# Two sets of edits together in a fused wavelet-attention and mixture-of-experts kernel: front stages and search rounds; tables, gathers and scatters

## The reference, cut to what matters

```
x = x + attn_block(layernorm(x));  x = x + moe(layernorm(x))        # both in f32
attn_block: two levels of depthwise 4-tap convolutions with stride 2 (low band by h_filter, high band by
  g_filter); linear attention with 16 heads of 8 channels on the lowest band (q = k = elu + 1); two levels
  of synthesis (repeat by 2, then depthwise 4-tap convolutions, low + high); layer norm of (x + low)
moe: h = 2048 x 128; scores = sigmoid(h @ gate_w.T)                 # 16 experts
  each expert takes the 256 tokens with its highest scores (top_k over the tokens, ids kept)
  xin = h[topk_ids]; eo = (silu(xin @ gw.T + gb) * (xin @ up_w.T + up_b)) @ down_w.T + down_b
  out = zeros.at[topk_ids].add(eo * topk_score) + shared           # 512 hidden columns per expert
  shared = (silu(h @ sh_gate.T) * (h @ sh_up.T)) @ sh_down.T        # 256 hidden columns, all tokens
```

## Time and profile before

| | us |
|---|---|
| median of 3 runs (242.78 to 243.35) | 243.33 |
| the profiled execution's own time | 241.03 |
| its span, first to last instruction | 239.3 |
| PE busy | 190.8 (80%) |
| DVE busy | 126.6 (53%) |
| POOL busy | 124.1 (52%) |
| ACT busy | 93.6 (39%) |
| POOL scatters L430, 32 of them | 50.9 |
| POOL gathers L418, 32 of them | 31.6 |

### The profile page before, as it was taken

How to read it: one execution, slowest core, us unless ns; L and a number is a source line. 1 busy time by engine, 2 the same in 40 slices (tenths; PEclk the granted TensorE clock), 3 DMA queues, 4 the chain that set the end, 5 groups by cost and what they waited for, 6 DMA issues and landing times.

```text
span 239.3 us, 3513 instructions
## 1 busy us (share of the span) xinstructions
PE 190.8 (80%) x1166; PEld 159.2 (67%) x1166; DVE 126.6 (53%) x450; ACT 93.6 (39%) x226; POOL 124.1 (52%) x155
## 2 busy tenths in 40 slices
PE   7369899999975886839578999999998888999100
PEld 7354787999862354527366899999988778889100
DVE  3679546489664788877833444444443433444000
ACT  1375301041979646611203444444444344344100
POOL 7310000035310434370987887787778877665660
PEclk9979999999996799976999999999999999999755
DMA  6999992000008300101022332333223333322331
GB/s 212 407 418 417 416 416 98 3 1 3 0 8 212 153 3 1 45 0 44 3 69 59 83 49 38 45 51 48 40 42 49 47 47 34 37 22 22 26 29 11
DMA packets 11584, 22.18 MB, mean 93 GB/s; under 512 B 1456, under 2 KB 8752, under 8 KB 11440
## 3 DMA queue, kind: packets, MB, share of 16 engines
q1 hardware_dynamic: 5936, 17.52, 19.2%
q0 software_dynamic: 5632, 4.46, 14.4%
HBM read 17.65 MB, written 4.33 MB: 92 GB/s over the span
## 4 chain that ended last, share of the span: by engine, by line
PE 39%; DMA 16%; DVE 13%; POOL 13%; issue 8%; ACT 7%; POOLq 1%; SPq 0%; DVEq 0%
DMA out_dram<-area,rows 12%; POOL out_dram L430 8%; PE bank L966 7%; PE bank L1215 5%; PE bank L1104 4%; PE bank L1216 4%; DVE junk L786 4%; PE bank L1198 4%; DMA x_tok<-in_x_dram 3%; PE bank L946 3%; POOL hT L418 2%; ACT hrow L463 2%; POOL sh_hid L404 2%; PE bank L1012 2%; DVE search L804 1%
## 5 line engine op out<-in xcount | busy, mean ns | idle before, releaser
L430 POOL DMA_INDIRECT out_dram<-area,rows x32 | 50.9, 1589 | 18.4 <-DMA out_dram<-area,rows 10.2
L912 DVE SCALAR_TENSOR_TENSOR area<-bank,consts,sgate 128x256 f32<-128x256 f32 x64 | 30.8, 481 | 34.9 <-ACT sgate L596 34.9
L596 ACT ACTIVATE sgate<-bank,consts 128x256 f32<-128x256 f32 x64 | 30.0, 468 | 45.9 <-PE bank L1216 45.9
L1215 PE MATMUL bank<-area,wT 128*128 128x256 f32 x128 | 39.4, 390 | 4.9 <-issue 4.0
L1198 PEld LDWEIGHTS bank<-wT,area 128*128 128x128 f32 x256 | 38.3, 191 | 3.2
L384 POOL TENSOR_TENSOR rstd<-var_eps,half_pow 128x4 f32<-128x4 f32 (+1 forms) x10 | 12.5, 1249 | 50.4 <-DVE var_eps L622 50.4
L1198 PE MATMUL bank<-wT,area 128*128 128x128 f32 x256 | 38.6, 275 | 0.0
L1216 PE MATMUL bank<-area,wT 128*128 128x256 f32 x128 | 38.1, 379 | 0.0
L418 POOL DMA_INDIRECT hT<-h_rows,rows x32 | 31.6, 986 | 9.5 <-issue 9.2
L404 POOL TENSOR_TENSOR sh_hid<-sh_up,sgate 128x128 f32<-128x128 f32 x32 | 16.9, 559 | 30.1 <-ACT sh_up L564 19.1
L1216 PEld LDWEIGHTS bank<-area,wT 128*128 128x128 f32 x128 | 24.4, 190 | 3.3
(11 more groups left out here) (181 smaller groups left out, 263.3 us busy)
## 6 DMA issues: line engine op xcount, KB each, us to landing
wT<-in_weights_dram SPq DMA_DIRECT2D x16, 768.0 KB, 18.1
h_rows<-hrow SPq DMA_DIRECT2D x2, 576.0 KB, 3.5
x_tok<-in_x_dram SPq DMA_DIRECT2D x2, 512.0 KB, 5.2
x_tok<-in_down_b_dram SPq DMA_DIRECT2D x1, 1024.0 KB, 6.7
out_dram<-x SPq DMA_DIRECT2D x4, 256.0 KB, 2.2
hT<-h_rows,rows POOLq DMA_INDIRECT x32, 2.6
out_dram<-area,rows POOLq DMA_INDIRECT x32, 3.4
sh_wT<-in_shared_dram SPq DMA_DIRECT2D x1, 384.0 KB, 7.4
```

The costliest lines, as they stand in the source:

```text
L430: pool.indirect_dma_start(out=out_rows, in_=eo[:, e % 2, c, :], in_offset=None, out_offset=bass.IndirectOffsetOnAxis(ap=rows[:, g, c, k:k ...
L596: act.activation(sgate_e[:, q % SGB, :], up_bank(q)[:, CAP:2 * CAP], ACT.Silu, bias=biasT[:, 1, j, e:e + 1]).then_inc(s_sil, 1)
L912: dve.scalar_tensor_tensor(hidden[:, e % 2, j, :], up_bank(q)[:, 0:CAP], biasT[:, 0, j, e:e + 1], sgate_e[:, q % SGB, :], ALU.add, ALU.mul ...
L1215: pe.matmul(up_bank(q)[:, 0:CAP], wT[:, e, 0, j, :], xselT[:, e % 2, :], start=True, stop=True)
```

## The change: what it does, and the diff

**Loads.** SP waits for the second half of x before it issues the shared weights and all that follows.

**Front.** The high band of level one is computed by PE for sequence 0 alone; DVE computes it for sequence 1 (`high1`, four operations, of the forms of L663 and L665). DVE finishes `h2p` before it waits for `kv`. PE's order changes: `add_xn` moves ahead, level one of the synthesis is done by sequence (`synth1_even(b)` in banks 4 and 7), and groups 0 and 1 of level two come before sequence 1's odd part. `turn_x1(0)` moves in between groups 2 and 3. The warm-up matmuls are (0, 8, 8, 0) in place of (8, 8, 2, 4). ACT makes `features` for group 0 alone.

**Search rounds.** The other 12 tiles of `hrow` are made by DVE, one in each of rounds 0 to 11 (`norm_tiles([4 + r], ...)`). `features_T` of groups 1 to 3 runs in rounds 3, 7 and 11, `keep_hT` in rounds 4, 8 and 12. SP stores each half of `hrow` when its tiles are there.

**Tables.** The slots are written in f16 and transposed with an f16 identity. `shared_down(2)` moves ahead of that transpose. POOL no longer multiplies or adds group 3 of the shared part: DVE multiplies it (`s_lasthid`, between `slot_rows(0)` and `own_expert(1)`) and adds it to x1 ahead of `keep_x(0)` (`s_lastbase`).

**Gathers and scatters.** POOL issues 10 chunks, then for each expert `scatter(e)` and behind it as many single chunks as `BETWEEN[e]` says.

```diff
+    AHEAD = 5
+    BETWEEN = (2, 2, 1, 2, 2, 1, 2, 2, 1, 2, 2, 1, 2, 0, 0, 0)
...
             load_x(1)
+            sp.wait_ge(s_x[1], 16)
             sp.dma_start(sh_wT[:, :, :], shared).then_inc(s_shw, 16)
...
             for b in range(NB):
-                sp.wait_ge(s_hna, 2 * (b + 1))
+                sp.wait_ge(s_hna, 1)
+                sp.wait_ge(s_hnv, 1 + 2 * b)
...
-            for n in range(LAST + 1):
+            for n in range(LAST):
                 for t in range(SHT):
...
+            shared_add(LAST - 1)
...
-            for e in range(GBUF - 1):
-                gather(e)
-                if e == 3:
-                    shared_add(LAST)
+            for e in range(AHEAD):
+                for c in range(CH):
+                    gather(e, c)
+            chunk = AHEAD * CH
             for e in range(E):
-                if e + GBUF - 1 < E:
-                    gather(e + GBUF - 1)
                 scatter(e)
+                for _ in range(BETWEEN[e]):
+                    gather(*divmod(chunk, CH))
+                    chunk += 1
...
             normalise_sum(2)
+            keep_x1T(1)
             features(0)
-            keep_x1T(1)
             normalise_sum(3)
-            features(1)
...
-            features(2)
             keep_hT(0)
-            features(3)
...
-                if r in (0, PERIOD, 2 * PERIOD):
-                    keep_hT(1 + r // PERIOD)
+                if r in (4, 8, 12):
+                    keep_hT(r // 4)
             keep_part(len(ROUNDS) - 1)
-            for part in range(4):
+            keep_down(LAST - 1)
+            for part in (0, 2):
                 keep_shared(LAST, part)
-            keep_down(LAST - 1)
-            keep_down(LAST)
...
+            def high1(k):
+                r, o = PHASE[k]
+                dst, src = h1p[:, 1, 1:N1 + 1], xp[:, r, 1, o:o + N1]
+                if k == 0:
+                    return dve.tensor_scalar(dst, src, taps[:, 4:5], None, ALU.mult)
+                return dve.scalar_tensor_tensor(dst, src, taps[:, 4 + k:5 + k], dst, ALU.mult, ALU.add)
...
                     dve.wait_ge(s_dve, step[0])
+                    if r < NT - 4:
+                        last = norm_tiles([4 + r], lambda i: hrow[:, i, 0:C], x1_t)
+                        if r % 4 == 3:
+                            last.then_inc(s_hnv, 1)
                     link(dve.scalar_tensor_tensor(base, ktab, ...))
...
-            slot_gt = score2[:, :]
+            slot_gt, slot_eq = slot_f[:, 0, :], slot_f[:, 1, :]
...
             slot_rows(0)
+            for t in range(SHT):
+                dve.wait_ge(s_shsil, SHT * LAST + t + 1)
+                dve.wait_ge(s_shu, SHT * LAST + t + 1)
+                dve.tensor_tensor(sh_hid[:, LAST % 2, t, :], bank[2 + t][:, :], sgate[:, t, :], ALU.mult).then_inc(s_lasthid, 1)
             own_expert(1)
...
+            dve.wait_ge(s_shout, LAST + 1)
+            last_x1 = x1[:, group(LAST), :].rearrange("p i c -> p (i c)")
+            dve.wait_ge(s_base, LAST)
+            dve.tensor_tensor(last_x1, bank[4][:, :], last_x1, ALU.add).then_inc(s_lastbase, 1)
             dve.wait_ge(s_db_in, 16)
             keep_x(0)
...
+            add_xn(0)
+            add_xn(1)
             pe.wait_ge(s_l2, 1)
...
+            pe.wait_ge(s_apa, 1)
+            synth1_even(1)
+            synth2_low(0)
+            synth2_high(1)
+            synth2_low(1)
             synth1_odd(1, h2p, 9)
-            pe.wait_ge(s_apa, 1)
             synth1_odd(1, ap_, 4).then_inc(s_up2, 1)
-            synth2_high(1)
-            synth2_low(0)
-            synth2_low(1)
-            for n in (2, 3):
-                synth2_high(n)
-                synth2_low(n)
...
+            synth2_high(2)
+            synth2_low(2)
+            turn_x1(0)
+            synth2_high(3)
+            synth2_low(3)
...
+            for t in range(4):
+                shared_down(LAST - 1, t)
             pe.wait_ge(s_pos, 1)
             for r in range(2):
-                pe.matmul(bank[5][:, r * P:(r + 1) * P], score2[:, r:256:2], ident[:, :], start=True, stop=False)
-                last = pe.matmul(bank[5][:, r * P:(r + 1) * P], sel[:, 4, r:256:2], ident[:, :], start=False, stop=True)
+                for k in range(2):
+                    last = pe.matmul(bank[5][:, r * P:(r + 1) * P], slot_f[:, k, r:256:2], ident_h[:, :], start=(k == 0),
+                                     stop=(k == 1))
             last.then_inc(s_posT, 1)
             for t in range(4):
-                shared_down(LAST - 1, t)
                 shared_up(LAST, t // 2, t % 2)
```

More of the change, by code:

```diff
@@ L408, in _, with gather @@
                     shared_add(n - 1)
-            def gather(e):
+            shared_add(LAST - 1)
+            def gather(e, c):
                 g, k = divmod(e, 8)
-                if e % 8 == 0:
+                if e % 8 == 0 and c == 0:
                     pool.wait_ge(s_rows, g + 1)
-                if e >= GBUF:
+                if e >= GBUF and c == 0:
                     pool.wait_ge(s_eo, CH * (e - GBUF + 1))
[L417 to L420, removed]
+                pool.indirect_dma_start(out=gath[:, e % GBUF, c, :], out_offset=None, in_=h_rows[:, :],
+                                        in_offset=bass.IndirectOffsetOnAxis(ap=rows[:, g, c, k:k + 1], axis=0),
+                                        ).then_inc(s_gath[e % GBUF], 16)
             def scatter(e):
@@ L942, in _ @@
             pe.wait_ge(s_diag, 1)
-            for b in range(NB):
-                pe.wait_ge(s_xp, 2 * b + 2)
-                for k, (r, o) in enumerate(PHASE):
-                    last = pe.matmul(bank[4 + b][:, :], diag[:, k, :], xp[:, r, b, o:o + N1], start=(k == 0), stop=(k == 3))
-                last.then_inc(s_h1, 1)
+            pe.wait_ge(s_xp, 2)
+            for k, (r, o) in enumerate(PHASE):
+                last = pe.matmul(bank[4][:, :], diag[:, k, :], xp[:, r, 0, o:o + N1], start=(k == 0), stop=(k == 3))
+            last.then_inc(s_h1, 1)
             def place(n, t):
@@ L979, in synth2_low, with synth1_even, synth1_odd @@
                 synth(n, range(4), r1p, 4).then_inc(s_up1, 1)
+            def synth1_even(b):
+                for k, o in TAPS[0]:
+                    last = pe.matmul(EVEN_BANK[b][:, 0:N2], diag[:, 9 + k, :], h2p[:, b, o:o + N2], start=(k == 0),
+                                     stop=(o == 2))
+                last.then_inc(s_up2h, 1)
+            def synth1_odd(b, band, d0):
+                for k, o in TAPS[1]:
+                    last = pe.matmul(bank[5 + b][:, 0:N2], diag[:, d0 + k, :], band[:, b, o:o + N2],
+                                     start=(d0 == 9 and k == 3), stop=(d0 == 4 and o == 2), skip_group_check=True)
+                return last
+            add_xn(0)
+            add_xn(1)
             pe.wait_ge(s_l2, 1)
@@ L1006, in _ @@
             last.then_inc(s_nd, 1)
-            add_xn(3)
-            synth2_high(0)
-            def synth1_odd(b, band, d0):
-                for k, o in TAPS[1]:
-                    last = pe.matmul(bank[5 + b][:, 0:N2], diag[:, d0 + k, :], band[:, b, o:o + N2],
-                                     start=(d0 == 9 and k == 3), stop=(d0 == 4 and o == 2), skip_group_check=True)
-                return last
+            synth2_high(0, range(2, 4))
             pe.wait_ge(s_h2, 1)
-            pe.wait_ge(s_h1a, 2)
-            for k, o in TAPS[0]:
-                last = pe.matmul(bank[4][:, :], diag[:, 9 + k, :], h2p[:, :, o:o + N2], start=(k == 0), stop=(o == 2))
-            last.then_inc(s_up2h, 1)
+            pe.wait_ge(s_h1a, 1)
+            synth1_even(0)
             synth1_odd(0, h2p, 9)
@@ L1072, in _ @@
             pe.wait_ge(s_gc, 1)
-            for g in range(LAST + 1):
+            for g in range(1, LAST + 1):
+                turn_x1(g)
+                router(g - 1)
                 stay_warm(WARM_T[g], bank[5])
-                turn_x1(g)
-                if g:
-                    router(g - 1)
             last = router(LAST)
```

99 lines of the change are left out of this document (60 added, 39 removed).

## The result

| | before | after |
|---|---|---|
| median, us | 243.34 (4 runs, 242.78 to 243.95) | 251.53 (4 runs, 248.71 to 256.22) |
| the profiled execution's own time | 241.03 | 251.9 |
| its span | 239.3 | 250.1 |

The ratio is 1.0297, with an interval of 1.0207 to 1.0388: slower, as forecast, and by more than forecast (forecast +4.0; measured +8.2 in the medians, +7.2 by the ratio). The two traces stand 10.8 apart, more than the medians, since the execution profiled before was shorter than each of the four runs in the table and the one after is the longest of the three that the ratio uses. What follows explains the traces.

A forecast was written before the change was run, and what follows sets the result against it. It took POOL's full queue of scatters and gathers to bound the longest stretch. Scatter 0 at -13.2, chain +12.0 and PE's clock +5.2 summed to +4.0, a median of 247.3 us, range 240.5 to 252.

The forecast's parts named there:

- Loads, front, scores: Start to ACT's first count: loads -1.7, synthesis -2.3, behind its end -2.6, together -6.6; features leaving ACT after the scores -2.85.
- Rounds: Search rounds: DVE tiles 1.0, copies 0.4 and edges 0.3 against a clock gain of 0.75; sum +1.0, bounds -1 and +4.5.
- a gain of 0.75: First three search rounds: PE sits idle less before them, so its granted clock is less low, -0.75.
- Tables: Last search round to PE's first expert matmul: f16 transposes, earlier rows and POOL's earlier first gather, -2.95.
- the bounds: Tables: -0.5, where PE's clock falls before shared_down(2), and -4.
- Scatter 0: Start of the first scatter: PE's first expert matmul at 115.75 plus 9.85 gives 125.6, 13.2 earlier.
- The chain: Scatter 0 onward: late gathers close a loop behind scatter 9; 103.5 against 91.5, +12.0, plus 5.2 for PE's clock.
- The clock term: Late expert steps: PE's clock halves in idle gaps, doubling its 1.75 in three of four steps; +5.2, bounds 0 and +7.
- together 9.1: Closed loop behind scatter 9: two scatters 3.82, landing 2.55, turn_x to bias 1.84, bias 0.42, ACT 0.4 and signals, 9.1.
- No starvation: Rival for the expert chain: late gathers land before PE asks; chain 90.5, 229 us in all; chance 0.10.
- Its clock stays up: Rival for the expert stretch: gathers starve PE but its clock holds; 242.1 us; chance 0.20.
- the third: Rival: front's gain mostly missing; tiles lengthen rounds by 0.3 each, shared_down(2) meets low clock; 252 us; chance 0.12.

The follow-up runs named there:

- experiment 6: SP's wait for the second half of x, alone in the kernel before: 241.67 us, ratio 0.9951; taken out of experiment 8's kernel: 230.78 us, ratio 0.9543.
- experiment 8: Experiment 1's kernel with nine warm-up matmuls on PE ahead of the first table, run twice: 228.07 us (ratio 0.947) and 229.61 us (0.9498).
- experiment 7: Experiment 1's kernel with features of groups 1 to 3 back on ACT and no DVE tiles in the rounds: 232.03 us, ratio 0.9596.
- experiment 2: The changed kernel with POOL's old order, 12 chunks ahead, then a scatter and two gathers per expert: 231.27 us, ratio 0.9544.
- experiment 5: The changed kernel, POOL's order untouched, with turn_x(e+1) issued one q later, behind the down ending expert e-1: 236.02 us, ratio 0.9801.
- experiment 1: The changed kernel with 12 chunks gathered ahead of scatter 0 in place of 10: 230.98 us, ratio 0.9484.
- experiment 3: The kernel before with only the new order of gathers and scatters (10 ahead, new BETWEEN): 259.92 us, ratio 1.0783.
- experiment 4: The changed kernel with 14 warm-up matmuls on PE ahead of its gather waits for experts 12 to 15: 246.11 us, ratio 1.0184.
- experiment 9: Experiment 8's kernel with a one-column POOL memset taking the waits ahead of scatter 0: 228.81 us, ratio 0.9485.

## Why the prediction was right in its mechanism and low in its sum

**Loads, front, scores: right, one size low.** Forecast: ACT's first count 6.6 + 2.85 = 9.45 earlier. It came at 63.41 in place of 74.08, 10.67 earlier, and the first compare 10.03 earlier:

```profile
62.11 0.40 ACT L553 ACTIVATE area<-bank 128x256 f32<-128x256 f32 x1 [1.03 <-PE bank L1129]
...
63.41 0.52 ACT L568 ACTIVATE below<-area,search 128x256 bf16<-128x256 uint16 x1
```

The scores started at 69.68 before, so 7.57 of it is the front's, against 6.6. DVE's second half of x came 1.80 earlier (forecast 1.7), the exponential 3.54 (21.30 in place of 24.84; forecast 1.7 + 0.95 = 2.65), and that is where most of the surplus lies. My sum treated the terms as independent, which experiment 6 refutes; it held since both edits were in.

**Rounds: forecast +1.0, measured +1.85.** The tiles cost what I took, 0.05 to 0.1 each on the mean: without a second stretch of half clock the rounds take 28.16 with them (experiment 8) and 28.54 - 1.2 without (experiment 7), some 0.8 for 12 tiles. Only the spread was other: 0.5 of it lies in the tenth step, where a tile and the operation behind it met POOL's operations. The rule of "Who interferes with whom" ("SBUF — State Buffer", the Trainium skill), which I had weighed for this term, is what those rows agree with: tiles that meet POOL are 0.58 long, the others 0.34. The remaining 1.1 of the 1.85 is a second stretch of half clock, in the rounds from 74.6 to 79.2 (2.52 and 2.02 where 1.72 and 1.64 are usual). I had booked the clock as a gain of 0.75. It did not come: the first round took 1.73 in place of 1.98, but the granted clock was 0.50 in it and 0.71 in the next, and the first three together took 5.95 against 5.92.

**Tables: forecast -2.95, measured -1.45.** Both parts came: with a warm-up the stage is 21.93, 2.75 below before. What ate 1.3 of it in the kernel after is mostly a late landing, for which my sum had no term. The second gather landed 4.14 behind its issue, against the median of 2.6, and PE, done with the shared part, waited for it:

```profile
112.22 4.14 DMA hT<-h_rows,rows
```

```profile
116.40 0.44 PE L1235 MATMUL bank<-ident,hT 128*128 128x128 f32 x2 [1.17 <-DMA hT<-h_rows,rows]
```

From the first gather to PE's first expert matmul it is 6.82 here and 5.74 in experiment 8's first trace. The half clock that I had put into the bounds was there too, though behind `shared_down(2)` and not ahead of it: PE has nothing from 102.5 to 104.8, and from 105.7 to 110 its granted clock is 0.50. But it was low before the change as well (0.50 from 106 to 110), and experiments 2 and 5, with the same low stretch (0.50 from 108 to 114 and from 105.9 to 111.9) and no late landing, have tables of 22.00 and 22.18. So here it cost 0.2 or so. Why that one landing was late was not tried. POOL's first gather followed its rows, as forecast; but 0.90 behind them, not 0.2 (rows written from 109.51 to 109.80, gather at 110.70).

**Scatter 0: forecast -13.2, measured -10.6.** Rounds 0.85, tables 1.5, less 0.6 from the earlier first compare, make PE's first expert matmul 1.77 later than forecast. The rest, 0.84, is the step from there to the scatter: 10.69 in place of 9.85. The first chunk was ready at 127.34, as long after PE as before; the scatter started at 128.21. Before, POOL was in the middle of its queue then, with 0.30 between two instructions, and I took that for what a waiting POOL would show too.

**The chain: forecast 103.5 + 5.2, measured 112.98.** The mechanism is right at every point: which step is the first long one, which is the longest, what ends PE's wait, and the fall of the clock. Experiments 1, 3, 5 and 4 show its cause (the chunks), its independence of the front, its lock (the place of `turn_x`) and its clock term. The clock term was right in sum, 5.36 against 5.2, by luck and not in its parts: all four steps pay, by 1.03 to 1.49 each, and not three by 1.75. The steps up to scatter 9 took 0.8 more than forecast, of landings that ended late (7.01 in place of 6.42 in one step, behind a scatter that landed after 4.81 where 3.4 is the median), the last two 0.1. What was mis-sized is the fixed part of the loop, "together 9.1": at the full clock it is 9.97 (experiment 4). Of the 0.87, 0.76 is again the start of POOL's indirect DMA, 0.81 behind the first chunk where I had put some 0.05 for signals. Over the four steps the loop without the clock's price took 40.86 where I had 37.7, 3.2 more.

Against the forecast the trace's span is 6.8 longer (250.1 against 243.3): 2.6 up to scatter 0 and 4.3 in the chain. Of this 3.9 is one term, POOL's start (0.84 at scatter 0, four times 0.76 in the loop); 1.5 are the tables (1.1 of it the late landing), 0.85 the rounds, 1.1 landings and small parts of the chain, and 0.6 goes the other way, from the front. In the medians a good third is given back, and that is luck: I had added 2.30 for the distance between the profiled execution and the median, and after the change the profiled one was above it. The median lies 0.5 below the upper end of the range.

**The rivals.** "No starvation" fell with the first late step. "Its clock stays up" fell with experiment 4's comparison: clock 0.74 in the window from 188 on where the warmed kernel has 1.00. Of the third neither reason came: the tiles did not cost 0.3 each, and `shared_down(2)` ran at a granted clock of 1.00 (94.29 to 98.00). The 0.85 and 1.5 that rounds and tables lost against the forecast have the causes above.

**What stays open.** Why a stretch of half clock falls in the rounds of some executions (74.6 to 79.2 in the kernel after, none there in experiments 5 and 9) was not tried. Nor was what an indirect DMA does in its 0.7 before it starts, nor why a wait for ACT or DVE brings it and a wait for a landing doesn't (the last section has the rows). Whether the warm-up in the tables is worth time and not only stage length is within the noise of these runs.

## What to carry to other kernels

When one in-order queue issues both the loads of a pipeline and its stores, compute for every store which load the consumer asks for before it can produce that store's data, and count how many loads stand ahead: a schedule that spreads loads between stores can look smoother and still close a loop of store, load, landing and compute. Two more loads ahead, or the consumer's wait moved behind the work that the store needs, opens it, the first in full and the second for the most part (chains of 90.92 and 97.93 against 112.98). What counted here was the number ahead and not the spread. And price a wait on a queue that was never idle before with what starting again costs there (0.8 in place of 0.30 here, where the wait was for a compute engine), not with the gap between two instructions of a full queue; the clock's fall in the new gaps comes on top.

## What the runs showed of the hardware

**An indirect DMA starts late when POOL waited for ACT or DVE.** It began 0.77 to 0.96 us behind the end of what it waited for (scatter 0: 127.34 to 128.21, late scatters: 205.31 to 206.12 and 202.83 to 203.64, first gather: 109.80 to 110.70). A memset in its place began after 0.13. In a full queue the gap between two such DMAs is 0.30. The length of the idle time does not set it: behind 6.55 us it was 0.78 (the kernel after, 217.49), behind 2.35 us 0.77 (experiment 3, 244.12 to 244.89), behind 1.90 us 0.86 (its scatter 0, 137.75 to 138.61). Behind 2.09 us of waiting for the landing of other scatters it was 0.26 (the kernel after, landed at 235.46, started at 235.72).

**What gaps cost PE.** Behind idle times of 2.7 to 4.9 us PE worked at a granted clock of 0.50 (1.2 GHz), in the first late turn only behind the transposes: in a full turn transposes, `up` and `down` took 3.29 in place of 1.78. Where its idle time was cut by small matmuls that write nothing of use, leaving 0.95 us idle, the clock stayed at 1.00 and the same work took 1.78:

```profile
200.20 0.44 PE L1238 MATMUL bank<-ident,hT 128*128 128x128 f32 x2 [0.95 <-DMA hT<-h_rows,rows]
```
